# Layer norms by statistics operations and a gated feed-forward stage spread over more engines, in a two-layer attention kernel on one core

## The reference, cut to what matters

```python
def _layernorm(x, axis=-1, eps=1e-05):
    m = jnp.mean(x, axis=axis, keepdims=True)
    v = jnp.var(x, axis=axis, keepdims=True)
    return (x - m) / jnp.sqrt(v + eps)
...
def bit_linear(x, w, b):
    gamma_x = jnp.clip(jnp.max(jnp.abs(x), axis=-1, keepdims=True), 1e-05, None)
    scale_x = 127.0 / gamma_x
    x_dq = jnp.clip(jnp.round(x * scale_x), -128.0, 127.0) / scale_x
    gamma_w = jnp.clip(jnp.mean(jnp.abs(w)), 1e-05, None)
    w_dq = jnp.clip(jnp.round(w / gamma_w), -1.0, 1.0) * gamma_w
    return jnp.einsum('bsd,hd->bsh', x_dq, w_dq) + b
```

## Time and profile before

| what | value |
|---|---|
| median of 3 runs | 6699.94 us |
| the profiled execution, its own time | 6694.85 us |
| its span | 6692.8 us |
| TensorE busy | 5788.9 us, 86% |
| VectorE busy | 5604.2 us, 84% |
| ScalarE busy | 4493.5 us, 67% |
| GpSimd busy | 3706.5 us, 55% |
| the four norms, first to last VectorE instruction | 22.4 us each |
| the gated stage, from the start of its norm at 6376.46 us to the end | 316.3 us |
| of it the loop over row tiles, from 6455.5 us | 237.3 us |

### The profile page before, as it was taken

One profiled execution on the slowest core, in us unless ns is written; L12 is line 12 of the kernel. 1 busy time (PEld: TensorE's weight loads), 2 busy tenths in 40 slices (PEclk: granted clock), 3 DMA queues, 4 the chain that ended last, 5 costly groups with the idle time before them and its releaser, 6 DMA issues. The chain is left out here.

```text
span 6692.8 us, 179938 instructions
## 1 busy us (share of the span) xinstructions
PE 5788.9 (86%) x64153; PEld 2456.4 (37%) x64160; DVE 5604.2 (84%) x8840; ACT 4493.5 (67%) x4358; POOL 3706.5 (55%) x3978
## 2 busy tenths in 40 slices
PE   2874999999999999999999999999969486999723
PEld 2651233333333333333333333333344353544411
DVE  4877999999999899899999989999963556777765
ACT  0660588988898899898889988988932012666401
POOL 2331488888788788788888878878820001000000
PEclk7995799999999999999999999999979697999866
DMA  1544101101101001011011011010010078877600
GB/s 58 124 121 125 18 9 23 21 8 26 18 11 25 15 16 25 10 21 22 10 24 20 9 27 18 11 25 14 15 36 0 17 291 197 117 110 113 97 29 10
DMA packets 176564, 315.49 MB, mean 47 GB/s; under 512 B 91731, under 2 KB 137812, under 8 KB 171042
## 3 DMA queue, kind: packets, MB, share of 16 engines
q1 hardware_dynamic: 175656, 303.45, 21.2%
HBM read 192.39 MB, written 113.07 MB: 46 GB/s over the span
## 5 line engine op out<-in xcount | busy, mean ns | idle before, releaser
L1163 DVE TENSOR_REDUCE a_mx<-PS 128x1 f32<-128x512 f32 x6620 | 4072.9, 685 | 235.9 <-PE PS L1047 232.3
L1134 ACT ACTIVATE a_e<-PS,a_sk 126x1024 f32<-126x1024 f32 x3264 | 3634.0, 1114 | 490.2 <-PE PS L1030 141.6
L901 POOL TENSOR_SCALAR a_p<-a_e 126x1024 f16<-126x1024 f32 x3264 | 3412.9, 1046 | 677.8 <-ACT a_e L1134 624.7
L1030 PE MATMUL PS<-a_Q,a_K 54*126 54x512 bf16 x6528 | 2109.9, 404 | 32.2 <-issue 23.0
L1047 PE MATMUL PS<-a_K,a_Q 48*128 48x512 bf16 (+1 forms) x6884 | 2106.7, 383 | 30.9 <-POOL a_p L866 30.6
L1074 PE MATMUL PS<-a_e,a_sel 126*32 126x256 f32 x26112 | 1994.1, 382 | 27.2 <-issue 27.2
L1030 PEld LDWEIGHTS PS<-a_Q,a_K 54*126 54x126 bf16 x6528 | 614.6, 131 | 1382.9 <-issue 1323.9
L1070 PE MATMUL PS<-a_p,a_V 128*32 128x256 f16 x13056 | 960.0, 284 | 14.6 <-ACT a_og L1115 10.5
L1070 PEld LDWEIGHTS PS<-a_p,a_V 128*32 128x32 f16 x13056 | 336.8, 93 | 1250.4 <-POOL a_p L901 1053.3
L1074 PEld LDWEIGHTS PS<-a_e,a_sel 126*32 126x32 f32 x26112 | 756.0, 110 | 37.1 <-issue 30.7
L2120 DVE TENSOR_REDUCE b_mx<-PS 128x1 f32<-128x512 f32 x803 | 504.4, 684 | 188.7 <-PE PS L2004 188.7
(11 more groups left out here) (330 smaller groups left out, 3435.9 us busy)
## 6 DMA issues: line engine op xcount, KB each, us to landing
b_K<-d_k SPq DMA_DIRECT2D x210, 200.1 KB, 6.2
a_K<-d_k SPq DMA_DIRECT2D x99, 400.2 KB
d_v<-v1v SPq DMA_DIRECT2D x9, 3328.0 KB, 10.3
b_V<-d_v SPq DMA_DIRECT2D x36, 832.0 KB, 12.4
d_k<-k_T SPq DMA_DIRECT2D x100, 252.0 KB, 4.1
d_k<-k1p SPq DMA_DIRECT2D x54, 400.2 KB, 7.0
a_V<-d_v SPq DMA_DIRECT2D x68, 204.0 KB, 2.8
d_v<-vq SPq DMA_DIRECT2D x17, 803.2 KB
```

Of the source, the lines that this page charges most:

```text
L901: g.tensor_scalar(p[0:rows, kk % RE, :], e[0:rows, kk % RE, :], 1.0, SHIFT, ALU.mult, ALU.add).then_inc(rounded, 1)
L1030: last = pe.matmul(self.PS[0:key_rows(s), e_bank(i, s) + y, :], Kb[0:E_ROWS, (i // NC) % 2, s * KT:s * KT + key_rows(s)], Qb[0:E_ROWS, i % ...
L1134: a.activation(e[0:r, kk % RE, :], self.PS[0:r, e_bank(i, s):e_bank(i, s) + 2, :], ACT.Exp, scale=skb[0:r, hb, s:s + 1]).then_inc(exp_done, 1)
L1163: v.tensor_reduce(mx[:, col:col + 1], bank, AX.X, ALU.max).then_inc(max_done, 1)
```

## The change

The norm no longer uses whole-tensor passes. For each of the 16 row tiles VectorE issues `bn_stats` over 256 columns (`norm_sums`), then 16 times `bn_aggr` on its six numbers, which gives mean and variance; after the root on ScalarE (`norm_root`) and the reciprocal, 16 `tensor_scalar` instructions subtract the mean and multiply in one pass (`norm_apply`). Inside each group of 16 there is no wait. ScalarE's squares are gone.

In the gated stage all three matrices have a tensor of their own and are loaded at the start, in one block with the norm. VectorE sums the magnitudes of all three between the two halves of the norm. The scaling and the addition of the rounding number are one ScalarE instruction for each matrix; subtracting that number, and the clip, are two GpSimd instructions for each matrix. In the loop the value half leaves PSUM by a ScalarE copy with scale, and GpSimd adds its bias in place; the output matmuls and `final` run one tile later than the transposes.

```diff
-                self.link(v, v.tensor_reduce(st[:, 0, :], self.x[:, :, :], AX.X, ALU.add), self.dv)
-                self.link(v, v.tensor_scalar(st[:, 1, :], st[:, 0, :], 1.0 / D, None, ALU.mult), self.dv)
-                v.tensor_tensor(xn[:, :, :], self.x[:, :, :], along(st[:, 1, :], 2, D),
-                                ALU.subtract).then_inc(centred, 1)
...
+    def norm_sums(self, v, nm):
+
+        for t in range(self.sh.NT):
+            self.mark(v.bn_stats(nm["parts"][:, t, :], self.x[:, t, :]), self.dv)
+        v.wait_ge(self.dv, self.count[id(self.dv)])
+        for t in range(self.sh.NT):
+            self.mark(v.bn_aggr(nm["mean_var"][:, t, :], nm["parts"][:, t, :]), self.dv)
+        v.wait_ge(self.dv, self.count[id(self.dv)])
+        v.tensor_scalar(nm["st"][:, 2, :], nm["mean_var"][:, :, 1], EPS, None, ALU.add).then_inc(self.var_ready, 1)
+
+    def norm_apply(self, v, nm, xn):
+
+        st = nm["st"]
+        v.wait_ge(self.std_ready, nm["now"])
+        self.link(v, v.reciprocal(st[:, 0, :], st[:, 3, :]), self.dv)
+        for t in range(self.sh.NT):
+            self.mark(v.tensor_scalar(xn[:, t, :], self.x[:, t, :], nm["mean_var"][:, t, 0:1], st[:, 0, t:t + 1],
+                                      ALU.subtract, ALU.mult), self.dv)
+        v.wait_ge(self.dv, self.count[id(self.dv)])
+
+    def norm_root(self, a, nm):
+
+        a.wait_ge(self.var_ready, nm["now"])
+        self.link(a, a.activation(nm["st"][:, 3, :], nm["st"][:, 2, :], ACT.Sqrt), self.ac)
+        a.sem_inc(self.std_ready, 1)
...
-            wf = self.sb(ctx, "wf", [P, 2 * F])
+            wf = self.sb(ctx, "wf", [P, 3, 2 * F])
...
+                @block.vector
+                def _(v):
+                    L = lambda ins: self.link(v, ins, self.dv)
+                    self.norm_sums(v, nm)
+                    for i in range(3):
+                        v.wait_ge(ld[i], 16)
+                        L(v.tensor_reduce(gw[:, i, 0:1], wf[:, i, :], AX.X, ALU.add, apply_absolute_value=True))
+                        L(v.tensor_scalar(gw[:, i, 1:2], gw[:, i, 0:1], 1.0, None, ALU.mult))
+                        v.sem_inc(part, 1)
+                    for i in range(3):
+                        v.wait_ge(summed, i + 1)
+
+                        L(v.tensor_scalar(gw[:, i, 2:3], self.PS[:, i, 0:1], 1.0 / (D * F), 1e-5, ALU.mult, ALU.max))
+                        L(v.reciprocal(gw[:, i, 3:4], gw[:, i, 2:3]))
+                        v.sem_inc(scale_ready, 1)
+                    self.norm_apply(v, nm, xn)
...
+                @block.scalar
+                def _(a):
+                    self.norm_root(a, nm)
+                    a.wait_ge(rounder, 1)
+                    for i in range(3):
+                        a.wait_ge(scale_ready, i + 1)
+
+                        a.activation(wf[:, i, :], wf[:, i, :], ACT.Identity, bias=rnd[:, 0:1], scale=gw[:, i, 3:4]).then_inc(shifted, 1)
+
+                @block.gpsimd
+                def _(g):
+                    g.memset(rnd[:, :], ROUND).then_inc(rounder, 1)
+                    for i in range(3):
+                        g.wait_ge(shifted, i + 1)
+                        g.tensor_scalar(wf[:, i, :], wf[:, i, :], ROUND, -1.0, ALU.subtract, ALU.max).then_inc(clipped, 1)
+                        g.wait_ge(clipped, 2 * i + 1)
+                        g.tensor_scalar(tern[i][:, :], wf[:, i, :], 1.0, None, ALU.min).then_inc(clipped, 1)
+                    g.wait_ge(clipped, 6)
...
                     for t in range(NT):
                         if t + 1 < NT:
                             gv(t + 1)
-                        rest(t)
+                        turn(t)
+                        if t >= 1:
+                            back(t - 1)
+                    back(NT - 1)
...
                 @block.scalar
                 def _(a):
-                    for t in range(NT):
+                    def front(t):
+                        a.wait_ge(gv_ps, t + 1)
+                        if t >= 2:
+                            a.wait_ge(h_ready, t - 1)
+                        a.activation(vt[:, t % 2, :], self.PS[:, 2:4, :].rearrange("p b n -> p (b n)"), ACT.Copy,
+                                     scale=st[:, 2, t:t + 1]).then_inc(v_taken, 1)
                         a.wait_ge(g_ready, t + 1)
                         a.activation(gt[:, t % 2, :], gt[:, t % 2, :], ACT.Silu).then_inc(g_act, 1)
...
+                @block.gpsimd
+                def _(g):
+                    for t in range(NT):
+                        g.wait_ge(v_taken, t + 1)
+                        g.tensor_tensor(vt[:, t % 2, :], vt[:, t % 2, :], vb[:, :], ALU.add).then_inc(v_ready, 1)
...
                     def back(t):
                         b = t % 2
                         v.wait_ge(g_act, t + 1)
+                        v.wait_ge(v_ready, t + 1)
                         L(v.tensor_tensor(gt[:, b, :], gt[:, b, :], vt[:, b, :], ALU.mult))
...
                         back(t)
-                        final(t)
+                        if t >= 1:
+                            final(t - 1)
+                    final(NT - 1)
```

More of the change, by code:

```diff
@@ L193, in _, with mark, norm_tensors, layernorm @@
                 self.link(a, a.activation(self.gates[:, :], raw[:, :], ACT.Tanh), self.ac)
-    def layernorm(self, ctx, tag, xn, extra_loads=None, keep=None):
-        nc, sh = self.nc, self.sh
-        NT = sh.NT
-        sq = keep if keep is not None else self.sb(ctx, f"ln_sq{tag}", [P, NT, D])
-        st = self.sb(ctx, f"ln_st{tag}", [P, 4, NT])
-        centred, squared, var_ready, std_ready = self.centred, self.squared, self.var_ready, self.std_ready
-        self.norms += 1
-        now = self.norms
-        with nc.Block() as block:
+    def mark(self, ins, sem):
+        self.count[id(sem)] = self.count.get(id(sem), 0) + 1
+        ins.then_inc(sem, 1)
+    def norm_sums(self, v, nm):
[18 more added lines that the diff above has]
+        a.sem_inc(self.std_ready, 1)
+    def norm_tensors(self, ctx, tag):
+        NT = self.sh.NT
+        self.norms += 1
+        return dict(st=self.sb(ctx, f"ln_st{tag}", [P, 4, NT]), parts=self.sb(ctx, f"ln_parts{tag}", [P, NT, 6]),
+                    mean_var=self.sb(ctx, f"ln_mv{tag}", [P, NT, 2]), now=self.norms)
+    def layernorm(self, ctx, tag, xn, extra_loads=None):
+        nm = self.norm_tensors(ctx, tag)
+        with self.nc.Block() as block:
             @block.sync
@@ L311, in loads @@
                 sp.wait_ge(ld, 32)
-            self.layernorm(ctx, "_a", xn, loads, keep=tmp)
+            self.layernorm(ctx, "_a", xn, loads)
             self.transpose_rows("_a", xn, xT, F32)
@@ L1464, in loads @@
                     sp.wait_ge(ld, 16 * 12)
-                self.layernorm(c1, "_m", xn, loads, keep=zm)
+                self.layernorm(c1, "_m", xn, loads)
                 self.transpose_rows("_m", xn, xT, F32)
@@ L1697, in loads @@
                 sp.wait_ge(ld, 32)
-            self.layernorm(ctx, "_b", xn, loads, keep=tmp)
+            self.layernorm(ctx, "_b", xn, loads)
             with nc.Block() as block:
@@ L2209, in gated_ffn @@
             ot = self.sb(ctx, "otf", [P, 2, D])
+            nm = self.norm_tensors(ctx, "_f")
             ld_b = self.sem(ctx, "ffn_biases")
[L2212 to L2217 removed]
@@ L2250, in gated_ffn, with _ @@
-            with nc.Block() as block:
+            ld = [self.sem(ctx, f"tern_loaded{i}") for i in range(3)]
+            part, summed, rounder = self.sem(ctx, "tern_part"), self.sem(ctx, "tern_sum"), self.sem(ctx, "tern_rounder")
+            scale_ready, shifted, clipped = (self.sem(ctx, n) for n in ("tern_scale", "tern_shifted", "tern_clipped"))
+            srcs = ("L1_ffn_gate_wT", "L1_ffn_val_wT", "L1_ffn_out_wT")
+            with nc.Block() as block:
+                @block.sync
+                def _(sp):
+                    for i, name in enumerate(srcs):
+                        cc = w[name].shape[0] // P
+                        sp.dma_start(wf[:, i, :].rearrange("p (c n) -> p c n", c=cc), w[name].rearrange("(c p) n -> p c n", p=P)).then_inc(ld[i], 16)
+                    for dst, src in ((gb, "L1_ffn_gate_b"), (vb, "L1_ffn_val_b"), (ob, "L1_ffn_out_b")):
+                        sp.dma_start(dst[:, :], on_all_rows(w[src])).then_inc(ld_b, 16)
+                    sp.wait_ge(ld_b, 48)
+                @block.tensor
+                def _(pe):
+                    for i in range(3):
+                        pe.wait_ge(part, i + 1)
+                        pe.matmul(self.PS[:, i, 0:2], self.onesf[:, :], gw[:, i, 0:2], start=True, stop=True).then_inc(summed, 1)
@@ L2285, in gv, with turn @@
                         ins.then_inc(gv_ps, 1)
-                    def rest(t):
+                    def turn(t):
                         pe.wait_ge(h_ready, t + 1)
@@ L2293, in rest, with back @@
                         ins.then_inc(h_turned, 1)
+                    def back(t):
                         pe.wait_ge(hT_ready, t + 1)
```

63 lines of the change are left out of this document (11 added, 52 removed).

## The result

The changed kernel took 6647.74 us (median of 4 runs, 6645.92 to 6652.62) against 6701.02 us before (4 runs). The ratio is 0.9926, 95% interval 0.9914 to 0.9939: 53 us faster. The forecast was 6656, 44 us faster; total and range held. The parts did not: the norms gave more, the stage ahead of the loop little, the loop much more than forecast.

What follows compares the result with a forecast made beforehand. Every norm and ternary step lies on the path, and the loop is one ring through all engines, none full. Savings of 17.4 + 23.9 + 2.3 = 43.6 us from 6699.94 gave 6656 us, range 6608 to 6680.

Steps and rivals of the forecast that it cites:

- The sum, 44 us: Whole kernel: savings of 17.4 in three norms, 23.9 ahead of the loop and 2.3 in the loop, 43.6 us.
- Norms, 5.8 us each: Norms `_a`, `_m` and `_b`: 16.6 us each against 22.4, 5.8 us saved in each.
- The loads in `_m` as what is late next: Norm `_m`: loads end about 14.7 us after the start and would be late if the norm came below that.
- GpSimd's ternary passes at 2.1 us: Ahead of the loop: six GpSimd passes over the ternary matrices, each at twice 1.046 = 2.1 us.
- rival D: Ahead of the loop and in it: GpSimd is slow and holds the port, 20 us slower, 6720; chance 0.03.
- The port excludes: Ahead of the loop and in it: GpSimd and certain VectorE instructions in SBUF exclude each other; saving ahead 23.9, not 36.7 us.
- The addition, 2.56 us from two small rows: Loop: GpSimd's bias addition over 1024 columns takes 2.56 us, starting 0.35 us ahead of VectorE's product.
- The loop, 0.1 us a tile: Loop: 14.5 us a tile instead of 14.64, as the product waits 2.2 us for GpSimd's addition; 2.3 us in all.
- `gv`: Loop: the next tile's gate and value matmuls, 2.9 us on average, put 0.2 us longer after the change.
- Rival A: Ahead of the loop and in it: the port costs nothing or GpSimd yields, 89 us saved, 6611; chance 0.13.
- B: Loop: the product starts first or the addition is short; 1.7 us a tile, 67 saved, 6633; chance 0.27.
- Rivals C and E: C, norms: statistics instructions are dear, 6692, chance 0.04. E, loop: later output matmuls save no wait, 6672, chance 0.03.

Runs made afterwards that it cites:

- experiment 7: Against the changed kernel: in all four norms VectorE waits for each small instruction before the next; 6658.8 us.
- Experiments 1 to 3: From the changed kernel: VectorE waits for GpSimd's six ternary passes, 6649.5 us; on that kernel, other operations in the passes, 6652.4 us; then six different forms, no time given.
- Experiment 5: Against the changed kernel: by a semaphore, GpSimd's bias addition of the next tile waits until VectorE's product of this tile is done; 6625.4 us.

## Why the prediction was right or wrong, point by point

- **The sum, 44 us, held (53 measured) because three wrong sizes made up for each other, and that is luck.** By the stretches the norms gave 9.3 us more than forecast, the stage ahead of the loop 19.2 less, the loop 16.3 more. Nothing in the total would have told.
- **Norms, 5.8 us each: too low.** The prices of one instruction were right for the statistics (0.42 against 0.409 us) and near for the others (aggregation 0.2 against 0.15, application 0.35 against 0.41). The step that failed is "16 make 6.8 us with gaps": I multiplied recorded durations. Issued without waits the sixteen are 0.33 us apart and the aggregations 0.07; experiment 7 puts the waits in and gets 7.35 and 3.43 us, near the 6.8 and 3.2 of the forecast, and 7.15 for the application, 1.6 above its 5.6. That the application came out at 5.26 in the change, near 5.6, is two errors that cancel: a price too low for one, and no overlap. The diff said it (`mark` instead of `link`), and I read it only as "no wait inside each group".
- **The loads in `_m` as what is late next**: right. The norm came below the 14.7 us named, and the loads ended the block. The 14.7 does not follow from its own working, though: 26 x 0.875 - 9.3 is 13.5, and the last busy slice of the earlier trace rows is the 27th, which gives 14.3. In the change the last load lands at 15.4.
- **GpSimd's ternary passes at 2.1 us: the term that was most wrong**, 7.1 and 5.4. I took L901's row by its name and size; it does product and sum, these do difference and maximum, or minimum alone. Experiments 1 to 3 show that it is not the turns with VectorE, nor maximum and minimum as such, nor the size, but the form. The six passes take 37.6 us in the change, where the forecast had 15; with 15 the rows would have been rounded at about 47 us, an estimate from the measured 69.5, even better than the 50.1 forecast, since the first pass starts at 17.2 instead of 20.5. The 7.1 us was the price of rival D (7.0 us by the slope of the small casts), which I gave 0.03 with the argument that L901 speaks against it. That its 7.0 meets the measured 7.1 is chance: a cast of that size takes 1.89 us. D itself did not come about, since its addition of 4.9 us was 2.34.
- **The port excludes** (the alternation ahead of the loop, the product behind the addition): right in both places. Three small steps, then one for each of six passes, then seven is just the count of the forecast ("3 + 6 of 16, the other 7"), at passes three times as long; the longest step took 7.17 us. The Trainium skill's rule (SBUF — State Buffer, "Who interferes with whom") says that the order of issue decides and that reduces stay out of it. Experiment 5 agrees: the product takes 3.01 or 1.23 us by order alone, the reduce 1.22 beside the addition. That GpSimd waits in turn when VectorE is first is shown only in the earlier trace rows; in experiment 5 a semaphore keeps it back.
- **The addition, 2.56 us from two small rows: near**, measured 2.34. The estimate of 2.3 from the GPSIMD Engine Reference of the Trainium skill (section 3.1) was nearer than my rows. Start ahead of the product: 0.35 forecast, 0.41 measured.
- **The loop, 0.1 us a tile: too low**, measured 1.17. The product's wait was 1.79 instead of 2.2; output matmuls behind the transposes gained 1.32 (2.14 to 0.82), not 1.11, since they start before the last transpose is recorded as ended; and the step "I put it 0.2 us longer" was wrong in sign. Gate row to `gv`'s first matmul was 9.85 + 1.69 = 11.54 us before and is 8.96 + 1.71 = 10.67 in the change, 0.87 less. `gv` itself was 14.64 - 11.54 = 3.1 us before (I had 2.9) and is 2.9 in the change (mean from its first matmul to the gate row, 3.66 in the third tile, 2.22 in the fourth, 2.98 in the late ones). The granted clock over the loop moved little, 0.62 before and 0.63 after. The +1.6 of the start was right (3.34 us between the first two gate rows, not 4.9).
- **The sign and the cases**: faster at 0.93 was right. Rival A (nothing excluded) and B (the product first) are refuted for the change itself; B's mechanism, made by hand in experiment 5, gave 14.64 - 11.81 = 2.83 us a tile against the 1.7 that B had: the scaling was held up by 0.3 us, not 0.6, the output matmuls gained 0.2 more, and `gv` took 2.6 us on average where B had 3.1. Rivals C and E are refuted by the norm's rows and by the 0.82 us between transposes and output matmuls.
